# A four-layer Fourier operator on one core: new job order in the sweeps, inverse products on 64-row array tiles, spectra kept in SBUF, last layer folded to one channel

## What is computed

```python
v = h @ p_w + p_b                                  # 3 -> 32 channels, B=128, 64x64
for i in range(4):
    x_ft = rfft2(v)                                # 24 x 12 modes are used
    out1 = einsum('bixy,ioxy->boxy', x_ft[:, :, :12, :12], W1)
    out2 = einsum('bixy,ioxy->boxy', x_ft[:, :, -12:, :12], W2)
    x1 = irfft2(out_ft)
    x2 = einsum('bcxy,cd->bdxy', v, w_w[i]) + w_b[i]
    v = batch_norm(x1 + x2)                        # over batch and pixels
    if i < 3: v = relu(v)
out = einsum('bcxy,cu->bxyu', v, q_w) + q_b        # 32 channels -> 1
```

## Time and profile before

| | |
|---|---|
| runs | 4268.0, 4279.57, 4272.75 us, median 4272.75 |
| profiled execution, span | 4267.0 us, 109552 instructions |
| PE busy | 3385.8 us, 79% |
| DVE busy | 2504.0 us, 59% |
| ACT busy | 1884.1 us, 44% |
| POOL busy | 482.7 us, 11% |
| DMA | 696.58 MB, mean 163 GB/s |
| largest groups on PE | line 940 953.1 us, line 665 374.8 us, lines 954 and 932 about 250 us each |

### The profile page before, as it was taken

The page is one execution under the profiler, slowest core; times in us unless marked ns, Lnnn a source line. Parts: engine busy times, 40 slices in busy tenths (PEclk is TensorE's granted clock), DMA queues, the critical chain, the costliest instruction groups (busy, mean ns, idle before and its releaser), DMA issues. The chain is left out here.

```text
span 4267.0 us, 109552 instructions
## 1 busy us (share of the span) xinstructions
PE 3385.8 (79%) x46184; PEld 2037.4 (48%) x46184; DVE 2504.0 (59%) x3890; ACT 1884.1 (44%) x3797; POOL 482.7 (11%) x337
## 2 busy tenths in 40 slices
PE   0679999937999993699999649999446778379999
PEld 0256666614666661366666326666312666223333
DVE  4567777736777772677777443333242676545555
ACT  0435555543555553355555344444311011046665
POOL 0331000023300000340000030000001344000000
PEclk7799999968999996899999879999778777689999
DMA  4267676658877774688777545444300221166775
GB/s 132 108 164 174 155 164 155 148 178 266 276 252 256 250 232 141 234 275 262 246 262 247 156 193 192 169 171 179 70 30 25 66 65 46 23 111 121 119 120 97
DMA packets 396803, 696.58 MB, mean 163 GB/s; under 512 B 174481, under 2 KB 317521, under 8 KB 379665
## 3 DMA queue, kind: packets, MB, share of 16 engines
q1 hardware_dynamic: 389282, 686.29, 56.2%
q10 hardware_dynamic: 7088, 3.95, 0.5%
HBM read 397.80 MB, written 292.34 MB: 162 GB/s over the span
## 5 line engine op out<-in xcount | busy, mean ns | idle before, releaser
L807 ACT ACTIVATE p_v<-p_ps,k_scale_bias 128x512 f32<-128x512 f32 x1024 | 787.9, 779 | 897.8 <-PE p_ps L940 839.5
L940 PE MATMUL p_ps<-k_idfty,p_t 128*128 128x256 f32 x4096 | 953.1, 386 | 0.0
L940 PEld LDWEIGHTS p_ps<-k_idfty,p_t 128*128 128x128 f32 x4096 | 757.5, 190 | 308.2 <-issue 214.6
L672 DVE STREAM_TRANSPOSE p_t<-p_ps 128x1024 f32<-128x1024 f32 x256 | 473.3, 1919 | 415.3 <-PE p_ps L665 415.3
L252 DVE STREAM_TRANSPOSE p_vt<-p_v 128x512 f32<-128x512 f32 x768 | 542.7, 711 | 269.9 <-ACT p_v L807 264.2
L815 ACT ACTIVATE p_j<-p_ps 128x512 f32<-128x512 f32 x768 | 447.4, 597 | 140.5 <-PE p_ps L954 140.5
L1859 DVE TENSOR_TENSOR x_ht<-x_ht,x_mask 128x384 f32<-128x384 f32 x512 | 268.5, 556 | 247.5 <-ACT x_ht L1833 245.4
L665 PE MATMUL p_ps<-p_yt,k_idftx 64*128 64x192 f32 x4096 | 374.8, 333 | 21.9 <-issue 21.9
L665 PEld LDWEIGHTS p_ps<-p_yt,k_idftx 64*128 64x128 f32 x4096 | 337.5, 190 | 108.8 <-issue 108.8
L1833 ACT ACTIVATE x_ht<-x_ph,x_b 128x384 f32<-128x384 f32 x576 | 303.1, 577 | 195.5 <-PE x_ph L1880 195.5
L232 PE MATMUL p_ps<-p_vt,k_dfty 32*32 32x512 f32 x6144 | 228.5, 602 | 100.4 <-issue 100.4
(11 more groups left out here) (233 smaller groups left out, 3388.5 us busy)
## 6 DMA issues: line engine op xcount, KB each, us to landing
field<-p_v SPq DMA_DIRECT2D x384, 512.0 KB, 10.6
p_v<-field SPq DMA_DIRECT2D x96, 2048.0 KB
y_spectrum<-m_y SPq DMA_DIRECT2D x24, 2048.0 KB, 7.6
p_y<-y_spectrum SPq DMA_DIRECT2D x128, 384.0 KB, 4.2
x_mask<-expert_weights SPq DMA_DIRECT2D x32, 1536.0 KB, 13.9
x_spectrum<-p_sp SPq DMA_DIRECT2D x384, 72.0 KB
m_raw<-x_spectrum SPq DMA_DIRECT2D x24, 1152.0 KB
k_mixw<-in_L_tok_fw_dram SPq DMA_DIRECT2D x16, 1152.0 KB
```

The source lines that it names most:

```text
L672: return nc.vector.transpose(st[:, q].rearrange("p x c -> p c x"), ps[:, 2 * q:2 * q + 2, :].rearrange("p j (c m) -> p c j m", m=16))
L807: nc.scalar.activation(v[:, b, at:at + CH], ps[:, half if last_layer else b % 2, g, :], ACT.Identity if last_layer else ACT.Relu, bias=bia ...
L940: ins = nc.tensor.matmul(ps[:, e, g, 256 * d:256 * d + 256], lines, K["idfty"][:, :], start=False, stop=True, skip_group_check=True)
```

## The change

- **Sweep.** `sweep_phase` replaces `field_phase` for layers 0 to 2. TensorE's order for job i is now pixels half 0 of i, y_product of i-1, pixels half 1, channels half 0 of the same job i, spectrum of i+1, channels half 1, x_product of i-1. Waits are split by bank: pixels half 1 waits for each evicted bank, channels half 1 and the next pixels half 0 for each squared bank. v has three buffers, spectrum tiles one.
- **Inverse along y** (was line 940): each product of 128 rows by 256 columns becomes two of 64 rows by 128 columns, one on each half of the array's rows, into different banks.
- **Inverse along x** (was 665): 64 output columns in place of 128 half filled with zeros, two results side by side; the accumulation over h is gone.
- **DVE**: pixels are turned in 4 instructions of 1024 columns in place of 8 of 512, modes in one of 768 in place of 4 of 192; modes and spectrum are written contiguously.
- **Squares** are written back into their PSUM bank in place of SBUF.
- **Spectra**: the modes go by four POOL copies per job from `sp` to `xm`, which stays in SBUF; `x_spectrum`, `raw` and the copies of mix_phase are gone for layers 1 to 3. POOL turns the weights in 32 smaller pieces, two per job from job 3.
- **Last layer**: mix_phase keeps its results in SBUF (`y_all`) and does not use POOL or DRAM; `last_phase` scales q_w by the batch-norm scale, contracts the spectrum to one channel, transforms it, and sums it with v times (w_w q_w) for all 128 images in eight PSUM banks.

```diff
 def inverse_x(nc, K, ps, yt, q):
     for t in range(2):
         for h in range(2):
             for j in range(2):
                 rows = slice(64 * j, 64 * j + 64)
-                out = ps[:, 2 * q + j, :].rearrange("p (c t k) -> p t c k", t=2, k=8)[:, t, :, 0:6]
-                ins = nc.tensor.matmul(out, K["idftx"][rows, t, h, :], yt[rows, 2 * q + h, :], start=(h == 0), stop=(h == 1), ...)
+                ins = nc.tensor.matmul(ps[64 * h:64 * h + 64, 2 * q + j, 192 * t:192 * t + 192], K["idftx"][rows, t, :],
+                                       yt[rows, :, 2 * q + h, :], start=True, stop=True)
...
# sweep_phase, SP
+            for i in range(n):
+                if i < 4:
+                    load_weights(eng, s, K, fw, layer + 1, i)
+                if i + 2 < n:
+                    spectrum_in(i + 2)
+                    load(i + 2)     # waits: store of i-1 landed, channels and pixel turns of i-1 done
+                store(i)            # waits: job i evicted
# ACT
+            for i in range(n):
+                evict(i, e, 0); evict(i, e, 1); squares(i, 1 - e, 0); squares(i, 1 - e, 1)
# DVE
+            for i in range(n):
+                pixels_turn(i - 1, 1); modes_turn(i - 2, 1 - e); spectrum_turn(i + 1)
+                rows_turn(i - 1, 1 - e); pixels_turn(i, 0); inverse_turn(i + 1, e)
# TensorE, pixels(i, e, half)
+                for g in range(G):
+                    if half == 1:
+                        pe.wait_ge(s.uo_ready, NCH * i + g + 1)
+                    elif i >= 1:
+                        pe.wait_ge(s.sq_done, NCH * i - G + g + 1)
+                    for a in range(4):
+                        nc.tensor.matmul(ps[C * a:C * a + C, e, g, :], weights[...], v[rows, b, col:col + CH], start=True, stop=False)
+                for q in range(2):
+                    pe.wait_ge(s.t_ready, 2 * i + q + 1)
+                    for d in range(2):
+                        for b1 in range(2):
+                            for h in range(2):
+                                rows, col = slice(64 * h, 64 * h + 64), 256 * d + 128 * b1
+                                ins = nc.tensor.matmul(ps[:, e, 2 * q + h, col:col + 128], lines, K["idfty"][rows, :], ...)
# TensorE, the sweep
+            for i in range(n):
+                pixels(i, e, 0)
+                y_product(i - 1, 1 - e)
+                pixels(i, e, 1)
+                pe.wait_ge(s.a2_ready, 2 * i)
+                channels(i, 1 - e, 0)
+                spectrum(i + 1, e)      # per pair of banks: evicted
+                channels(i, 1 - e, 1)   # per bank: squares of half 0 done
+                pe.wait_ge(s.t_ready, 2 * i + 4)
+                x_product(i - 1, e)
# last_phase
+            for k in range(n):                                   # SP, five buffers
+                if k >= NV:
+                    eng.wait_ge(s.px_done, (k - NV) // 2 + 1)
+                eng.dma_start(v[k % NV], V[order[k]]).then_inc(u_in[k % NV], 16)
+            for m in range(9):                                   # PE: spectrum to one channel, 4 matmuls of 512 columns each
+            ...  # 4 DMAs to DRAM, 8 back (ACT's queue), 8 matmuls along x, copies, 1 DMA out, 8 back
+            def products(k):                                     # two jobs at a time
+                for bank in range(8):
+                    for e in range(2):
+                        nc.tensor.matmul(ps[C * t:C * t + C, bank, :], w_px[:, m, :], v[(k + e) % NV][:, CH * bank:CH * bank + CH],
+                                         start=(m == 0), stop=(m == 7))
+            pe.wait_ge(s.wq_ready, 6); pe.wait_ge(s.lx_ready, 2); pe.wait_ge(s.lx_ready_v, 2)
+            for k in range(0, n, 2):
+                products(k)
+                if k == 10:
+                    spectra()                                    # waits for the last 8 DMAs, 64 matmuls of 64 columns
```

More of the change, by code:

```diff
@@ L341, in _ @@
             for half in range(2):
-                for g in range(G):
-                    turn_pixels(nc, vt, px, half, g).then_inc(s.vt_ready, 1)
+                for pair in range(2):
+                    turn_pixels(nc, vt, px[:, :], half, pair).then_inc(s.vt_ready, 1)
             dve.wait_ge(s.fy_done, 1)
@@ L366, in _, with mix_phase @@
             transform_x(nc, K, ps[:, 1], at).then_inc(s.fx_done, 1)
-def mix_phase(nc, sems, tag, K, B, xsp, ysp, par, layer, first, last, grid_ft):
+def mix_phase(nc, sems, tag, K, B, isp, ysp, par, layer, first, last, grid_ft):
     s = sems
@@ L395, in mix_phase, with result @@
         block = ctx.enter_context(nc.Block())
+        def result(n):
+            return y_all[:, n] if last else yx[:, n % 2]
         @block.sync
@@ L402, in mix_weights, with next_weights @@
                     eng.dma_start(K["wbd"][rows, 0, rows], par["w_w"][layer]).then_inc(s.w_in, 16)
+            def next_weights(eng):
+                for g in range(G):
+                    rows = slice(C * g, C * g + C)
+                    eng.dma_start(K["wbd"][rows, 1, rows], par["w_w"][layer + 1]).then_inc(s.par_in, 16)
             def parameters(eng, g):
                 rows = slice(C * g, C * g + C)
-                if not last:
-                    eng.dma_start(K["wbd"][rows, 1, rows], par["w_w"][layer + 1]).then_inc(s.par_in, 16)
                 for name in ("w_b", "bn_g", "bn_b"):
@@ L903, in _ @@
[L903 to L911 removed]
+                at_least(dve, s.xm_a, 4 * i)
@@ L978, in project @@
-            def project(i, b):
-                pe.wait_ge(s.uo_ready, NCH * i + NCH)
-                pe.nop(nofuse=True)
-                for half in range(2):
-                    for g in range(G):
-                        at = 1024 * g + CH * half
-                        ins = nc.tensor.matmul(ps[32 * g:32 * g + G, 1, half, :], qbd[:, :], v[:, b, at:at + CH], start=True, stop=True)
-                ins.then_inc(s.hq_done, 1)
-            def body(i, b, r, last):
-                e = b % 2
-                later = not (isinstance(i, int) and i == 0)
-                pixels(i, b, r, 0)
-                if not last_layer and later:
-                    channels(i - 1, (b + 3) % 4, 1 - e, 0)
-                pixels(i, b, r, 1)
-                if not last_layer and later:
-                    channels(i - 1, (b + 3) % 4, 1 - e, 1)
-                if not last:
-                    spectrum(i + 1, 0 if last_layer else e)
-                if last_layer:
-                    project(i, b)
-                else:
-                    if later:
-                        x_product(i - 1, 1 - e)
-                    y_product(i, e, last)
-                    if last:
-                        channels(i, b, 1, 0)
-                        channels(i, b, 1, 1)
-                        x_product(i, 1)
```

828 lines of the change are left out of this document (486 added, 342 removed).

## The result

The changed kernel takes 3741.48 us, the median of 4 runs (3720.97 to 3761.31), against 4271.24 us before: a ratio of 0.876 (95% interval 0.872 to 0.880). The forecast was 3575 us, the range 3400 to 3750. The direction is right and most parts are; the gain came out at 530 us where 698 were forecast. The profiled execution has a span of 3739.5 us.

What follows compares the result with a forecast made beforehand. It took TensorE's chain to bound the sweep job. Profile 4267 + 5 (image phase) - 300 (sweeps) - 68 (mixing) - 337 (last layer) = 3567, 3573 with 6 around it, stated as 3575 us; range 3400 to 3750.

Steps and rivals of the forecast that it cites:

- Bound and direction: Sweeps: TensorE busy 588 of 645 us, so shortening its chain shortens the job; chance of a faster kernel 0.96.
- Blocks on PE: TensorE's products in a sweep job, priced block by block after the change: 13.3 us in sum.
- Rival 4: Sweep: weight loads bound the halved inverse products, 0.216 us a pair; job 18.9 us, +177, total 3750; chance 0.05.
- The ring: Sweep job: TensorE and ACT wait for each other in a cycle through evictions, squares and products, 16.7 us a job.
- I take 17.0, with 0.3 for hand-overs: Sweep: the job falls from 19.38 to 17.0 us, upper bound 18.2; 74 us a layer over 31 jobs.
- start and tail: Sweep time outside its 31 jobs: 44 us in place of 73, with 26 of the 29 counted.
- Rival 1: Sweeps: data transfers bound the job at 18.5 us, 4.6 MB at 248 GB/s; +140, total 3715; chance 0.12.
- Rival 3: Sweeps: TensorE's pauses drop its clock to the 1.2 GHz level, job 24.7 us, +716, total 4310; chance 0.03.
- Mixing: Layers 1 and 2: mixing starts at once without loading and turning spectra, 35.2 us each less 1; -68 together.
- Last layer: Mixing 48, constants 5, last phase 218: 271 us in place of 608, so -337.
- Rival 5: Last layer: small spectrum transfers wait among 16 KB packets, products start at 90 for 45; +45, total 3620; within forecast's 0.66.
- Image phase: Image phase: weights turned in 96 smaller pieces cost 5 us more (0 to 8).

Runs made afterwards that it cites:

- run 1: Changed kernel with the channel products as 4 full-array products per half in place of 16 on 32x32 tiles: 3985.72 us.
- Run 7: Changed kernel with the inverse product along y on all 128 rows, zero-padded, so no two run at once: 3902.84 us.
- run 10: Changed kernel with only the stores of layers 1 and 2 cut to a quarter of the columns, loads whole: 3620.59 us.
- run 8: Changed kernel with the x product started on half the images, waiting for the second inverse turn only then: 3654.82 us.
- light runs: Two runs of the changed kernel with stores of layers 1 and 2 cut to a quarter: loads cut too, 3605.67 us; loads whole, 3620.59 us.
- runs 2 and 11: Changed kernel with empty TensorE instructions added that turned out not to be there, 3674.82 us; and changed kernel unedited once more, 3691.72 us.
- run 9: Changed kernel with the split x product, loads and stores paced over the job, and a filler product in the update loop: 3621.17 us.
- run 3: Changed kernel with both loads and stores of layers 1 and 2 cut to a quarter of the columns: 3605.67 us.
- run 12: Changed kernel with split x product, paced transfers and update-stage filler, its stores cut by image in place of by 32-partition group: 4706.11 us.

## Why the prediction was right, and where it was off

- **Bound and direction: right.** TensorE's chain set the job, and shortening it shortened the job.
- **Blocks on PE: right.** Inverse along y 1.99 us (forecast 1.95), along x 1.5 (1.6; the row is in run 1), x product 1.56 (1.5), channels 1.16 (1.07) in the first half, 2.56 in the second, with its waits. The direct products take 1.45 to 1.83 (1.25), since they wait bank by bank for evictions or squares. Rival 4 (weight loads bound the halved products, 0.216 a pair) is out: it wanted 3.5 us for the block, and the 16 pairs take 1.99, or 0.124 each. The Trainium skill, "TensorE: Matmul & The Clock Gate", part 3, has it that a weight load overlaps a product in flight only on another row group. The trace does not agree, if a load is as long as the prediction takes it: each half of the rows gets new weights for each of its 16 products, and load and stream one after the other would be those 3.5 us.
- **The ring: right in sum, less so in cause.** 16.4 us for the 16.7 worked out; four evictions are 2.79 for 3.2, squares 0.59 in PSUM for 0.58. Run 7 says that PE counts for more in it than I had it.
- **The step that failed: "I take 17.0, with 0.3 for hand-overs", the mean job.** It is 18.3, just past the upper bound of 18.2. 93 x 1.3 = 121 us, which is the 123 missing in the sweeps; start and tail are near the forecast (614 - 31 x 18.4 = 44, for 47). In its place: about 1.3 us a job in layers 1 and 2 that go when the stores are cut (18.4 and 18.3 in the mean for 17.0 and 17.1 in run 10). 0.8 of it is time in which PE stands, nearly all of it behind late instruction packets; the rest isn't traced, and it is not the clock, which is no better in run 10. The 0.6 from there to the shortest job I put down to the clock that falls after the pause for the inverse turn; run 8, which took the pause away, showed it only in layers 0 and 2, so this is not shown. The forecast's list had each engine and DMA queue but this one.
- **The total: inside the range with some luck.** Of the 172 us that the profile is above the forecast (3739.5 for 3567), 123 are the sweeps, and 67 the update stage, which is chance from run to run; 16 came back in the last layer, mostly by loads that were faster than the one row that I had priced them by.
- **Rival 1 (transfers bound the sweep, job 18.5)** has the number and the cause in part, not the mechanism. DMA was at 0.87 and 0.88 in layers 1 and 2, not 0.95, and no product waited for v; in the light runs the gaps inside groups go. Layer 0, with 154 GB/s, has the same mean job, which bandwidth can't explain.
- **Rival 3 (the clock falls)** came true in small: 0.94 for 0.97 in the sweeps.
- **Mixing: right.** -70 for -68; the first product starts 0.9 us after the barrier (843.30), for 35 before.
- **Last layer: 16 us better than forecast.** Mixing 55.9 with the constants for 53. In the last phase the products of the fields start 42 us in (2300.69), for 45, and the loads run at 431 GB/s, for 372:

```profile
2290.00:2300.00 10.00, 2.84 (x16) 0.80 (x16) 0.63 (x2) 0.56 (x2) 0.00 (x0) 0.50 0.13 34
...
2320.00:2440.00 120.00, 98.59 (x526) 31.21 (x524) 0.00 (x0) 0.00 (x0) 0.00 (x0) 0.93 1.01 431
```

  That is 4.87 us a load; 27 x 0.77 = 21 less, about the 19 by which 199 is under 218. The Trainium skill, "DMA: Bandwidth & Descriptors", section Bandwidth, has 425 GB/s for 16 MB, measured on a single core, and the trace of 2 MB loads back to back agrees (431). The 358 that the section gives is a core's share when both cores of a domain stream; this kernel runs on one. The one gap before the first products is there (2290 to 2300). Rival 5 is out: the small transfers came back 20 us after the contraction.
- **Image phase: +11 for +5.** The 96 pieces take 0.30 us each and start every 0.36: 35 us of DVE.
- **Token stages "unchanged": wrong by 67 us**, without any edit there. The profiled run fell on a slow update stage; the other three of the first series have a mean clock of 0.859 to 0.862 and may have too. With the stage at 141 us the kernel is at 3670 to 3690, as in runs 2 and 11.

## What to carry to other kernels

When an edit makes TensorE's instructions shorter, count them per us, and look what the transfer engines carry at that time: in the unrolled sweep 250 instructions were 5.8 us of work, and their packets came late while 2 MB were stored per job. The sign is idle time inside a group of one line, put down to "issue", with a packet of the instruction queue just before; storing less takes it away (run 10), so does giving a packet's worth of instructions more time (run 7, though it costs more than it gives), and spreading the transfers made the sweeps shorter (run 9). Before a theory of the clock is acted on, look at the granted clock of a run that takes its cause away: here it stayed as it was when the gaps went (run 10) and hardly moved when the pause went (run 8).

## What was not expected of the hardware

- One packet of instructions late is 0.5 to 4.9 us of TensorE, though the packet itself takes 1.0 to 1.1 us on its engine, in the light runs as in the others.
- With the stores cut to a quarter, instructions come in time (run 10); cutting the loads besides changes nothing (run 3: 570 and 578 us for 570 and 574).
- The update stage, the same code and instruction counts, takes 140.7, 150.6, 187.9 or 209.0 us by when the clock rises.
- The same 2 MB stored with another outer dimension goes at 105 GB/s (run 12).
